# Four sandwich layers on one core: side work of stage 2 handed over bank by bank and moved to other steps, and six transposes of attention moved by two chunks

## The reference, cut to what matters

```python
x = x + layernorm(attn0(layernorm(x)))       # stage 1: x is 2 x 1024 x 512, 16 tiles of 128 rows
x = x + layernorm(ffn0(layernorm(x)))        # stage 2: hidden = sigmoid(x w1q) * (x w2q), then hidden w3q
x = x + layernorm(attn1(layernorm(x)))       # stage 3: 16 heads of 32, 4 key/value heads, causal
x = x + layernorm(ffn1(layernorm(x)))        # stage 4: silu gate, 2:4 sparsity, down

# stage 3, before its softmax:
q = x @ q_w.T ; k, v = split(x @ kv_w.T)
oe, oo = te*cos - to*sin, te*sin + to*cos    # rotary turn of q and k: even and odd features
p = softmax(q k^T / sqrt(32) + mask) ; out = (p v) @ c_w.T
```

## Time and profile before

| | us |
|---|---|
| median of three runs | 1407.97 (1405.64 to 1408.61) |
| the profiled execution, its whole time | 1406.8 |
| its span in the profile | 1405.1 |
| TensorE busy | 1333.8 |
| VectorE busy | 976.9 |
| ScalarE, GpSimd busy | 665.3, 694.0 |

### The profile page before, as it was taken

One profiled execution on the slowest core, in us unless ns is written; L12 is line 12 of the kernel. 1 busy time (PEld: TensorE's weight loads), 2 busy tenths in 40 slices (PEclk: granted clock), 3 DMA queues, 4 the chain that ended last, 5 costly groups with the idle time before them and its releaser, 6 DMA issues.

```text
span 1405.1 us, 19463 instructions
## 1 busy us (share of the span) xinstructions
PE 1333.8 (95%) x7206; PEld 912.5 (65%) x7206; DVE 976.9 (70%) x1959; ACT 665.3 (47%) x1153; POOL 694.0 (49%) x836
## 2 busy tenths in 40 slices
PE   6989999999989899989999999999999999999998
PEld 5875445555455455554555447787888888888886
DVE  5998575755657776667666534688668766886687
ACT  6664333232313554445555585545454645455442
POOL 2576131421313323224234256685678768866863
PEclk9999999999999999999999999999999999999999
DMA  9100210203213121133021213322224232432300
GB/s 332 73 1 1 75 60 16 83 8 98 75 45 98 50 51 50 35 88 128 21 77 53 91 63 141 127 90 91 90 90 150 103 112 90 153 141 91 118 32 30
DMA packets 46270, 116.86 MB, mean 83 GB/s; under 512 B 3420, under 2 KB 4448, under 8 KB 42336
## 3 DMA queue, kind: packets, MB, share of 16 engines
q1 hardware_dynamic: 45104, 114.31, 24.1%
q10 hardware_dynamic: 1072, 1.31, 0.3%
HBM read 92.28 MB, written 23.07 MB: 82 GB/s over the span
## 4 chain that ended last, share of the span: by engine, by line
PE 67%; DVE 24%; ACT 5%; issue 3%; POOL 1%; DMA 0%; POOLq 0%; DVEq 0%; ACTq 0%
PE PS L1731 65%; DVE cm L661 5%; DVE SM L677 2%; DVE PS L870 2%; DVE SM L673 2%; PE PS L1740 1%; DVE tm L661 1%; DVE hm L670 1%; ACT EX L1301 1%; DVE hm L661 1%; DVE SM L678 1%; DVE hd L670 1%; ACT ws_g L1118 1%; DVE qb L667 1%; DVE SM L667 1%
## 5 line engine op out<-in xcount | busy, mean ns | idle before, releaser
L1301 ACT ACTIVATE EX<-PS 128x512 f32<-128x512 f32 (+3 forms) x384 | 170.8, 493 | 139.5 <-PE PS L1731 137.8
L1534 POOL TENSOR_TENSOR ws_g<-rw,ws_g 128x512 fp32r<-128x512 f32 x64 | 136.4, 2131 | 127.6 <-ACT ws_g L1118 127.6
L1534 POOL TENSOR_TENSOR SM<-SM 128x1 f32<-128x1 f32 x128 | 82.1, 642 | 224.1 <-DVE SM L667 221.2
L870 DVE CUSTOM_DVE_ANT_0 PS<-PS,MW 128x128 f32<-128x128 f32 (+3 forms) x256 | 122.6, 503 | 64.2 <-PE PS L1731 63.7
L1731 PE MATMUL PS<-KG,QG 96*128 96x512 f32 (+3 forms) x384 | 134.9, 381 | 20.7 <-DVE SM L870 7.8
L1650 POOL TENSOR_SCALAR_AFFINE_SELECT EX<-EX 128x128 f32<-128x128 f32 x256 | 75.0, 303 | 158.5 <-ACT EX L1301 156.1
L1503 ACT ACTIVATE ab<-hm 128x512 f32<-128x512 f32 x64 | 40.5, 633 | 207.6 <-DVE hm L661 207.6
L1731 PE MATMUL PS<-QG,KG 98*128 98x512 f32 (+3 forms) x384 | 131.5, 378 | 3.3 <-ACT EX L1301 2.9
L1731 PE MATMUL PS<-ws_d,HH 128*128 128x512 f32 x528 | 125.7, 390 | 0.3 <-DVE HH L661 0.3
L1731 PEld LDWEIGHTS PS<-QG,KG 98*128 98x128 f32 x384 | 69.8, 191 | 72.5 <-issue 46.1
L661 DVE TENSOR_TENSOR hm<-PS,sl 128x512 f32<-128x512 f32 x64 | 44.0, 688 | 103.5 <-PE PS L1731 61.1
(11 more groups left out here) (205 smaller groups left out, 2788.5 us busy)
## 6 DMA issues: line engine op xcount, KB each, us to landing
rw<-in_L_ffn_w_gate SPq DMA_DIRECT2D x16, 1024.0 KB, 5.1
rw<-in_L_ffn_w_up SPq DMA_DIRECT2D x16, 1024.0 KB, 5.1
rw<-in_L_ffn_w_down SPq DMA_DIRECT2D x16, 1024.0 KB, 7.1
QG<-qs SPq DMA_DIRECT2D x48, 256.0 KB, 4.3
raw<-in_L_ffn_w SPq DMA_DIRECT2D x3, 2816.0 KB, 11.6
qs<-stg SPq DMA_DIRECT2D x16, 512.0 KB, 3.5
xA<-xs SPq DMA_DIRECT2D x2, 2048.0 KB, 7.6
ys<-xA SPq DMA_DIRECT2D x4, 1024.0 KB, 4.3
```

The lines of the kernel that those rows point to most:

```text
L870: last = e.tensor_tensor_reduce(out=p, in0=p, in1=MW[:, 512 - k1 + k0:512], scale=1.0, scalar=BIG, op0=ALU.add, op1=ALU.max, accum_out=m1)
L1301: e.activation(EX[:, n % 16, 0:W], PS[:, score_bank(n), 0:W], ACT.Exp, scale=ISQ, bias=0.0).then_inc(S["ex"], 1)
L1534: return e.tensor_tensor(out, a, b, op)
```

## The change

It has five parts.

1. A bank of a unit counts as free when the two products that read it are made: `rope` of units 0 to 7 becomes `rope_products(y, par)` (even x cos and even x sin into the two result tiles; odd x sin into `vt`, odd x cos into `RD`) and `rope_sums(y)` (the difference and the sum). `freed` names the new semaphore `rb` for both banks of a unit. The copy of V in ScalarE waits for all rotary sums that use `vt` up to then.
2. In VectorE's program a step's maxima (`between`) come right behind `hd`; the cast and the remainder of `hd` (`halves2`) come behind them.
3. The pieces `t3` 0 to 3 and units 0, 1 and 2 stand one step earlier (15, 16, 17, 19, 21 instead of 16, 17, 18, 20, 22), with the statistics and normalisations that feed them.
4. The weight transposes `c` 0 and `c` 1 stand at steps 18 and 20 instead of 16 and 21.
5. In attention, h 2 to 7 stand five chunks behind their last unit's, not three.

```diff
-        jobs.update({14: ("k", 0), 15: ("v", 0), 16: ("c", 0), 21: ("c", 1), 22: ("c", 2), 23: ("c", 3)})
+        jobs.update({14: ("k", 0), 15: ("v", 0), 18: ("c", 0), 20: ("c", 1), 22: ("c", 2), 23: ("c", 3)})
...
-        for n, more in ((16, [("t3", 0), ("t3", 1)]), (17, [("t3", 2), ("t3", 3)]), (18, whole(0)), (20, whole(1)),
-                        (22, whole(2)), (24, value(0)), (25, [("VT", 0)]), (26, [("t3", 4), ("t3", 5)]),
+        for n, more in ((15, [("t3", 0), ("t3", 1)]), (16, [("t3", 2), ("t3", 3)]), (17, whole(0)), (19, whole(1)),
+                        (21, whole(2)), (24, value(0)), (25, [("VT", 0)]), (26, [("t3", 4), ("t3", 5)]),
...
-        stat3 = {i: n for i, n in zip(range(12), (14, 14, 15, 15, 24, 24, 25, 25, 35, 35, 36, 36))}
-        norm_3 = {i: n for i, n in zip(range(12), (15, 15, 16, 16, 25, 25, 26, 26, 36, 36, 37, 37))}
+        stat3 = {i: n for i, n in zip(range(12), (13, 13, 14, 14, 24, 24, 25, 25, 35, 35, 36, 36))}
+        norm_3 = {i: n for i, n in zip(range(12), (14, 14, 15, 15, 25, 25, 26, 26, 36, 36, 37, 37))}
...
-                behind[last + 3].append(("h", x // 48 * 2 + x % 48 // 32))
+                behind[last + 5].append(("h", x // 48 * 2 + x % 48 // 32))
...
-            if u[0] == "u" and u[1] >= 8:
-                return "ue", 2 * u[1] + u[2] - 15
-            return {"t3": ("xT3", u[1] + 1), "u": ("rp", 2 * u[1] + 2), "V": ("vt", u[1] + 1), "VT": ("va", u[1] + 1),
+            if u[0] == "u":
+                return ("ue", 2 * u[1] + u[2] - 15) if u[1] >= 8 else ("rb", 2 * u[1] + u[2] + 1)
+            return {"t3": ("xT3", u[1] + 1), "V": ("vt", u[1] + 1), "VT": ("va", u[1] + 1),
...
+            def rope_products(y, par):
...
+                w.wait_ge(S["pj"], 2 * y + par + 1)
+                if par == 0:
+                    w.wait_ge(S["ql"], max(0, 2 * y - 2))
+                    tt(rotated(y, 0), p, cs, ALU.mult)
+                    tt(rotated(y, 1), p, sn, ALU.mult).then_inc(S["rb"], 1)
+                else:
+                    w.wait_ge(S["vtp"], min(h, 2))
+                    w.wait_ge(S["rp"], 2 * y)
+                    tt(vt[:, :], p, sn, ALU.mult)
+                    tt(RD[:, :], p, cs, ALU.mult).then_inc(S["rb"], 1)
+
+            def rope_sums(y):
+                w.wait_ge(S["rb"], 2 * y + 2)
+                tt(rotated(y, 0), rotated(y, 0), vt[:, :], ALU.subtract).then_inc(S["rp"], 1)
+                tt(rotated(y, 1), rotated(y, 1), RD[:, :], ALU.add).then_inc(S["rp"], 1)
...
                 up2(n)
+                for t in between[n]:
+                    event(t)
+                halves2(n)
...
-                for t in between[n]:
-                    event(t)
...
-                w.wait_ge(S["rp"], 6)
+                w.wait_ge(S["rp"], min(16, 6 * h + 6))
                 cp(vt[:, :], PS[:, bank3(("V", h)), :]).then_inc(S["vt"], 1)
```

More of the change, by code:

```diff
@@ L44 @@
 d_rr0 d_rr1 d_cs mv5 rs5 tma tp5 hi5 xT3 vone
-pj ue rp qh ql d_w0 d_w1 d_k0 d_k1 d_k2 d_k3 d_q00 d_q01 d_q10 d_q11 vj vt vtp va
+pj ue rb rp qh ql d_w0 d_w1 d_k0 d_k1 d_k2 d_k3 d_q00 d_q01 d_q10 d_q11 vj vt vtp va
 sx mxr nm mtp mtl d_m0 d_m1 st ex sel pvd oe de rd oo d_xc cwh cwl
@@ L807, in up2, with halves2 @@
                 stt(hd2[:, u, :], PS[:, 5, :], HS / XS, sg2[:, u, :], ALU.mult, ALU.mult).then_inc(S["hd"], 1)
+            def halves2(n):
+                u = n % 2
                 w.wait_ge(S["hd"], n + 1)
@@ L831, in split3 @@
                          xT3(h, 1)[:, :, i % 4 * 128:(i % 4 + 1) * 128], 1.0, "xT3")
+            def rope_products(y, par):
+                h = y // 3
+                cs, sn = COS[:, h % 2 * 512:(h % 2 + 1) * 512], SIN[:, h % 2 * 512:(h % 2 + 1) * 512]
+                p = PS[:, bank3(("u", y, par)), :]
+                w.wait_ge(S["d_cs"], 32)
+                w.wait_ge(S["pj"], 2 * y + par + 1)
[12 more added lines that the diff above has]
+                tt(rotated(y, 1), rotated(y, 1), RD[:, :], ALU.add).then_inc(S["rp"], 1)
             def rope(y, pars):
@@ L836, in rope @@
                 sl = slice(h % 2 * 512, (h % 2 + 1) * 512)
[L837 to L840, removed]
+                p0, p1 = pt[y - 8][:, 0, :], pt[y - 8][:, 1, :]
                 cs, sn = COS[:, sl], SIN[:, sl]
-                B = vt[:, :] if h == 0 else RD[:, :] if y < 8 else tm4[:, 2, :] if y == 8 else n3[:, 0, :]
+                B = tm4[:, 2, :] if y == 8 else n3[:, 0, :]
                 w.wait_ge(S["d_cs"], 32)
@@ L850, in rope @@
                     A = rotated(y, par)
-                    w.wait_ge(S["pj"] if y < 8 else S["ue"], 2 * y + 1 if y < 8 else 2 * y - 15)
+                    w.wait_ge(S["ue"], 2 * y - 15)
                     w.wait_ge(S["ql"], max(0, m - 3))
                     tt(A, p0, cs if par == 0 else sn, ALU.mult)
-                    w.wait_ge(S["pj"] if y < 8 else S["ue"], 2 * y + 2 if y < 8 else 2 * y - 14)
+                    w.wait_ge(S["ue"], 2 * y - 14)
                     w.wait_ge(S["rp"], m)
@@ L886, in event @@
                     split3(t[1])
-                if t[0] == "u" and t[2:] == (1, 1) and t[1] < 8:
-                    rope(t[1], (0, 1))
+                if t[0] == "u" and t[3] == 1 and t[1] < 8:
+                    rope_products(t[1], t[2])
+                    if t[2] == 1:
+                        rope_sums(t[1])
                 if t[0] == "m":
```

## The result

| | before | after |
|---|---|---|
| median of 20 runs each (lowest) | 1411.36 us (1404.93) | 1399.42 us (1391.68) |
| ratio, with its 95% interval | | 0.9923 [0.9906, 0.9939] |
| the profiled execution | 1406.8 | 1398.8 |
| its span | 1405.1 | 1397.1 |
| stage 2: its first matmul to the first exponential | 325.1 | 316.1 |

The account below looks back on a forecast made before the run. TensorE was taken as the bound, losing time in waits for VectorE. Stage 2 8.9, waits 2.1 and 0.3, clock 3.0 sum to 14.3 us: 1406.8 becomes 1392.5, stated as 1393.5 for the median; range 1388 to 1400 (8 in 10).

Parts of the forecast that it names:

- 3.9 + 0.4 + 4.8: Stage 2 gains in us: four rotary-bank waits (3.9) and an `x` tile wait (0.4) by part 1, six maximum-bank waits (4.8) by part 2.
- the two waits of parts 3 and 4: Stage 2: TensorE's waits at t3 1 (1.6 us) and t3 3 (1.0) go, 3.0 us with surcharge.
- (a): Step 15: t3 1, moved there, newly waits for VectorE's remainder of `v` 0; a loss of 1.95 us, bounds 0 to 2.6.
- (b): Step 23: without unit 2 in step 22 the normalisation is no longer hidden; 1.3 us lost in two waits, bounds 0.8 to 1.6.
- surcharge on each wait: TensorE's waits: each costs 0.21 us more than its bracket shows; 13 stage 2 waits make 12.1 us, not 9.4.
- The waits of part 5: Attention: h 7's wait for `negm` goes (2.1 us), h 3 and h 4 give 0.3 together, h 1 keeps its wait.
- With the wait filled by the weighing, I expect no fall, and count 3.0: Attention at h 7: the half-clock stretch of 6.8 us disappears with the wait; 3.0 of its 3.4 us are gained.
- Part 5 as a whole: Attention: 2.1 us for the wait at h 7, 0.3 for h 3 and h 4, 3.0 for the clock, 5.4 us.
- The rival that the clock falls all the same round h 7: Attention: thin work and a new phase still bring the fall; gain 11.3 us, time 1396.7; chance 0.2.
- The sign by which it would be wrong: Attention: the forecast is wrong if its mean clock falls under 0.99; one of three such signs named.
- rival of multiplying falls: Step 15 and attention: remaining waits each bring a half clock at 3.0 us apiece; five make it slower, 1411.5; chance 0.02.

Follow-up runs that it names:

- e12: The changed kernel with parts 3 and 4 undone, so parts 1, 2 and 5 alone: 1399.60 us, ratio 0.9929 to before; stage 2 took 315.2 us.
- e8: The changed kernel with unit 2 back in step 22 and the remainder of `v` 0 ahead of the halves in step 15: 1391.98 us, ratio 0.9885 to before.
- e3: The kernel before with part 5 alone (h 2 to 7 five chunks behind): 1408.05 us, ratio 0.9990 to before.
- e11: The changed kernel with eight extra overwritten matmuls in step 20, so attention comes 1.7 us later: 1398.87 us, ratio 0.9927 to before.
- e15: e14 with four filler matmuls ahead of h 1: 1393.98 us, ratio 0.9900 to before.
- e13: The kernel before with eight overwritten filler matmuls ahead of h 7's wait: 1407.56 us, ratio 0.9993 to before.
- e5: The kernel before with part 1 alone: 1400.74 us in one run; stage 2 took 321.1 us.
- e2: The kernel before, unedited, timed again: 1409.07 us, ratio 0.9996 to before.
- e4: The changed kernel with part 5 undone, so parts 1 to 4 alone: 1403.04 us, ratio 0.9941 to before.
- e6: The kernel before with part 2 alone: 1404.36 us in one run; stage 2 took 320.2 us.
- e14: e8 with h 3 back at three chunks and GpSimd waiting in stage 4, from step 10 of each 16, for VectorE's comparisons: 1390.05 us, ratio 0.9875 to before.
- e1: The changed kernel, unedited, timed again: 1395.02 us, ratio 0.9905 to before.
- e7: The kernel before with parts 3 and 4 alone: 1412.86 us in one run; stage 2 took 326.7 us.
- e9: The changed kernel with GpSimd in stage 4 waiting for VectorE's comparisons at steps 11, 27, 43 and 59: 1394.97 us, ratio 0.9905 to before.

## Why the prediction was right and where it was wrong

- **Stage 2: 9.0 us for 8.9, the mechanism right, the closeness in part luck.** In the forecast's terms: 9.1 for parts 1 and 2 (3.9 + 0.4 + 4.8), 3.0 for the two waits of parts 3 and 4, less 3.25 for (a) and (b). Measured: 9.9 (e12), 3.0, less 3.9 (e8). Two misses of 0.8 and 0.6 cancel. Parts 1 and 2 give 1.0 more together than one by one, which the forecast's sum of single terms has no place for. (a) is right, 1.98 for 1.95. (b) was sized too low, 2.26 for 1.3, because it was read off step 12, where the sigmoid does not stand behind a unit's split and the cast does not run beside GpSimd's. A surcharge on each wait was needed: by brackets alone part 1 would be 3.3 and part 2 3.5, where 4.0 and 4.9 were measured.
- **Parts 3 and 4 are a loss as they stand.** The forecast's own terms said so, 3.0 - 1.95 - 1.3 = -0.25, and e12 measures -0.9.
- **The waits of part 5: right in kind.** h 3, h 4 and h 7 no longer wait, h 1 does, and m 101 waits 0.35 for V 3. From chunk 128 to 144 the profiles without part 5 take 22.3 to 22.6 us (seven), those with it 18.8 without a fall of the clock there (six) and 19.8 to 20.0 with one (e3, e11, e12, e15). With a fall of 3.4 us in both, the wait at h 7 was thus worth 22.3 - 19.9 = 2.4 (forecast 2.1). But chunks 144 to 160 then take 19.4 us for 18.8, so 1.8 is what is left at chunk 160. For h 3 and h 4, forecast 0.3: chunks 48 to 64 lose 18.0 - 17.6 = 0.4 and chunks 64 to 80 gain 18.55 - 17.70 = 0.85.
- **The step that failed: "With the wait filled by the weighing, I expect no fall, and count 3.0".** In the profile of after there is no fall at h 7, as forecast. Over the profiles a fall stands near h 7 in 7 of 7 without part 5 and in 4 of 10 with it, so in these it is rarer but not gone, and in e13 it stands there with the wait filled, so the reason given does not hold. The price was too high as well: about 1.8 us where 3.0 were counted. The 3.0 came from one fall of 6.8 us. In chunks 128 to 160 a fall of 3.4 costs 1.2 to 1.4 more than none (39.2 to 39.4 against 38.1, with part 5), and one of 6.8 costs 41.6 - 41.1 = 0.5 more than one of 3.4 (before and e5 against e2, e4, e6 and e13); the 1.8 is an estimate from these two. A fall of 3.4 elsewhere, e14 against e15, cost 38.6 - 37.2 = 1.4 (chunks 64 to 96) and 31.1 - 29.5 = 1.6 (160 to 192). For chunks 128 to 160 the wait and the clock together were forecast at 5.1 us; before and after differ there by 41.6 - 38.0 = 3.6 (1.8 for the wait and 1.8 for the clock), the means of the seven and the ten profiles by 2.9. At h 7 TensorE waits for VectorE anyway: in e13 the eight fillers and the fall put h 7 1.4 us later than in before (counted from chunk 128), and chunk 144 came 0.3 earlier. Working out the price as missing clock times length takes TensorE for the bound where the earlier trace rows show it waiting.
- **Part 5 as a whole: 2.5 us by the profiles, forecast 5.4.** The mean of attention is 394.8 us over the seven profiles without it and 392.2 over the ten with it; timed, e3 gives 1.4, e4 2.5 against after and 5.1 against e1. With 9.0 of stage 2 that makes 10.4 to 14.1, with 11.5 by the means of the profiles, against 10.9 measured. The rival that the clock falls all the same round h 7 has the nearest number (11.3), but not by its mechanism: in the profile of after the clock does not fall there. Its attention lacks 3.4 of the forecast 5.4 us in two places, 1.5 in chunks 128 to 160 and 2.0 in chunks 0 to 16, where the long fall stands.
- **The base was drawn from one execution.** The forecast took its 14.3 from 1406.8, which lay under before's medians: 1411.36 (20 runs), and 1410.26, 1407.89, 1408.89 and 1408.51 beside the experiments. From there the same gain ends at 1394 to 1397.
- **The sign by which it would be wrong came, for another reason.** The mean clock of attention is 0.98, under the 0.99 named. The cause is the 17.1 us at half clock from 436.0 on, a stretch that part 5 does not touch. Chunks 0 to 16 take 22.0 us with it and 19.4 in e1, where the fall lasts 6.8, and 20.0 in before. The forecast's sum has no term for falls that come anew; only its rival of multiplying falls, at 0.02, has. The 3.5 us lost in stage 4 are not in it either; there before and after drew one and two long comparisons.

What stays open: why a fall of the clock begins where it does. The profiles of attention come in two kinds. Those with falls in the middle (at 540 to 553 us, near h 7, and with part 5 again at 622 to 635) take 394.5 to 396.1 us (e2, e3, e4, e6, e11, e12, e15), the others 393.0 to 393.6 without part 5 (before, e5, e13) and 389.2 to 391.1 with it (six); e7, with a fall of 10.2 us at 603, stands apart at 397.4. What part 5 is worth hangs on the kind. Behind chunk 16 the second kind takes 372.5 to 373.0 us without it and 368.6 to 369.1 with it (370.6 and 370.8 in e9 and e1, which have a fall near 476), 3.4 to 4.4 us better. The first kind takes 374.4 to 374.5 without it and 374.6 to 375.1 with it, so nothing is gained there, and the further fall at 622 to 635 alone costs 1.6. Which kind an execution is decides as much as the edit. Whether part 5 makes the first kind rarer can't be said from 17 profiles (3 of 7 without it, 4 of 10 with it).

The Trainium skill, "TensorE: Matmul & The Clock Gate", section "What's actually happening", has the monitor's window free of the kernel's phase. The traces are in line with it: two executions of one program had falls of 17.1 us at 436.0 (after), and of 6.8 us at 436.0 and 3.4 at 477.0 (e1). No run here shows the phase itself.

## What to carry to other kernels

A wait that TensorE has on a full turn of banks is worth its bracket and about 0.2 us, and such terms summed to within about 1 us of 9 here, with two misses that cancelled; where two waits stand in one step, expect the two cures together to give more than one by one. A fall of the clock is priced worse: give it a full price only where TensorE is the bound, and no certainty that it goes with the wait beside it. Before a piece is moved a step, ask what it covered in the step that it leaves (here the normalisation of a row group), what its readers on the other engines then hold up in the step that follows (here the sigmoid), and who reads the bank two places earlier in the step that it enters. Take the base of a forecast from many runs, not from the profiled one, and read an unedited stage in several executions before its difference is explained by the edit.

## What the runs showed of the hardware that was not expected

A comparison of VectorE with two inputs in SBUF (128x1536) beside five products of GpSimd without a gap took either 2.1 to 2.6 us or 7.6 to 8.2 (e2 and before are one program). In the long form it began within one product, lost to the next at all four boundaries between the five, and ended 1.6 us behind the last. In the short form the two engines took turns, and GpSimd's products grew from 1.30 to 2.81 us. The Trainium skill, "SBUF — State Buffer", section "Who interferes with whom", says that a VectorE instruction with both inputs in SBUF contends with a GpSimd instruction that reads SBUF. These rows agree, and add that VectorE can lose several times in a row, at 3.0 us of the kernel each time in groups 2, 6 and 10.

With the falls of the clock in attention (5 us between its two kinds) and two such comparisons (6 us), executions of one program lie more than 10 us apart, so single profiles don't order two programs: e3's profiled span, 1411.1, is 8.0 us over e2's, 1403.1, while their timed ratios are 0.9990 and 0.9996.
